# Feed-forward weights of two turns converted, and a third turn's loaded, in the stage before

## What is computed

```
x = layernorm(x + L0_attn(x))             # a two-directional state space mixer
x = layernorm(x + L0_xattn(x, ctx))       # cross attention, 16 query heads, 4 key heads of 96
x = layernorm(x + L0_ffn(x))              # gated feed-forward, quantized weights
x = layernorm(x + L1_attn(x))             # causal self attention, 32 heads of 16
x = layernorm(x + L1_xattn(x, ctx))       # cross attention, 32 query heads, 8 key heads of 128
x = layernorm(x + L1_ffn(x))              # linear layer with routed low-rank terms

def L0_ffn(x):                            # 512 -> 1792 -> 512, scales in groups of 128 rows
    W = (imatrix - zeros) * scales        # for gate, up and down; integers 0 to 15
    return (silu(x @ W_gate) * (x @ W_up)) @ W_down
```

## Time and profile before

| | |
|---|---|
| median of 3 runs | 1649.45 us (1648.58 to 1652.18) |
| the profiled execution, its own time | 1650.77 us |
| its span, from the first to the last instruction | 1649.0 us |
| granted clock of TensorE, mean | 0.983 |
| first cross attention, main loop | about 247 to 527 us |
| feed-forward stage | about 528 to 754 us |

### The profile page before, as it was taken

One profiled execution on the slowest core, in us unless ns is written; L12 is line 12 of the kernel. 1 busy time (PEld: TensorE's weight loads), 2 busy tenths in 40 slices (PEclk: granted clock), 3 DMA queues, 4 the chain that ended last, 5 costly groups with the idle time before them and its releaser, 6 DMA issues. The chain is left out here.

```text
span 1649.0 us, 29540 instructions
## 1 busy us (share of the span) xinstructions
PE 1552.9 (94%) x10984; PEld 1290.7 (78%) x10984; DVE 951.0 (58%) x1693; ACT 798.9 (48%) x2426; POOL 768.0 (47%) x624
## 2 busy tenths in 40 slices
PE   6999999999998779998999889999999999999997
PEld 4777888888886557876777678888888888888875
DVE  3947503333356777778677835555555555555656
ACT  3342324444443445445988734454455445445532
POOL 3403215343321779763533527655455545554413
PEclk9999999999999899999999999999999999999999
DMA  6100200010101743204000021201101011010001
GB/s 211 39 1 1 58 20 21 21 38 5 53 1 46 230 134 128 90 1 122 1 2 27 27 91 39 65 26 39 35 31 52 17 49 39 27 33 14 1 1 51
DMA packets 61777, 77.84 MB, mean 47 GB/s; under 512 B 12168, under 2 KB 41348, under 8 KB 61636
## 3 DMA queue, kind: packets, MB, share of 16 engines
q1 hardware_dynamic: 61172, 74.63, 14.4%
q0 software_dynamic: 464, 1.32, 0.3%
HBM read 73.85 MB, written 2.10 MB: 46 GB/s over the span
## 5 line engine op out<-in xcount | busy, mean ns | idle before, releaser
L1152 POOL TENSOR_TENSOR xa_rs<-xa_ms,minus_half 128x5 f32<-128x5 f32 x64 | 74.8, 1168 | 160.5 <-DVE xa_ms L1423 160.3
L1158 POOL TENSOR_TENSOR xa_prob<-xa_prob,xa_inv 128x512 f32<-128x512 f32 x64 | 66.7, 1042 | 139.0 <-DVE xa_inv L1390 139.0
L766 POOL TENSOR_TENSOR xa_prob<-xa_prob,xa_inv 128x1024 f32<-128x1024 f32 x32 | 60.7, 1895 | 140.8 <-DVE xa_inv L1029 140.8
L1418 DVE TENSOR_REDUCE xa_ssq<-pre 128x4 f32<-128x512 f32 x64 | 43.9, 686 | 134.4 <-ACT pre L1354 134.4
L1368 ACT ACTIVATE xa_prob<-xa_prob,xa_peak 128x128 f32<-128x128 f32 x256 | 99.7, 391 | 41.9 <-DVE xa_peak L1434 41.9
L101 PE MATMUL late_bank<-late_q_hi,xT_hi 128*128 128x512 f32 x284 | 117.9, 415 | 0.0
L1745 DVE SCALAR_TENSOR_TENSOR ff_acc<-ff_ring,ff_sT,ff_acc 128x512 f32<-128x512 f32 x140 | 100.6, 747 | 21.1 <-ACT ff_acc L1699 14.5
L103 PE MATMUL late_bank<-late_q_lo,xT_hi 128*128 128x512 f32 x284 | 112.6, 397 | 0.0
L102 PE MATMUL late_bank<-late_q_hi,xT_lo 128*128 128x512 f32 x284 | 112.5, 396 | 0.0
L1354 ACT ACTIVATE pre<-late_bank 128x512 f32<-128x512 f32 x64 | 38.2, 597 | 141.3 <-PE late_bank L103 141.3
L1985 POOL TENSOR_TENSOR pre<-pre,sa_inv 128x1024 f32<-128x1024 f32 x32 | 63.7, 1989 | 92.0 <-DVE sa_inv L2192 92.0
(11 more groups left out here) (414 smaller groups left out, 4929.9 us busy)
## 6 DMA issues: line engine op xcount, KB each, us to landing
pre<-in_wq SPq DMA_DIRECT2D x8, 1024.0 KB, 5.7
late_raw_o<-in_wo SPq DMA_DIRECT2D x8, 1024.0 KB, 5.3
ff_dn_q<-in_down_w SPq DMA_DIRECT2D x7, 512.0 KB, 3.9
ff_dn_z<-in_down_z SPq DMA_DIRECT2D x7, 512.0 KB, 5.0
ff_dn_s<-in_down_s SPq DMA_DIRECT2D x7, 512.0 KB, 5.8
pre<-in_wq SPq DMA_DIRECT2D x16, 192.0 KB, 3.4
pre<-in_wo SPq DMA_DIRECT2D x16, 192.0 KB, 3.8
pre<-in_xT SPq DMA_DIRECT2D x4, 512.0 KB, 8.1
```

Source lines behind the costliest of these rows:

```text
L766: pool.tensor_tensor(prob[:, t % 3, :, :], prob[:, t % 3, :, :], bc(inv[:, t % 3, :], 2, [P, Q, KEYS]), ALU.mult).then_inc(s["norm"], 1)
L1152: pool.tensor_tensor(rs[:, :], ms[:, :], m.minus_half[:, 0:Q + 1], ALU.pow).then_inc(s["rs"], 1)
L1158: pool.tensor_tensor(prob[:, u % 2, :, :], prob[:, u % 2, :, :], bc(inv[:, u % 2, :], 2, [P, Q, S]), ALU.mult).then_inc(s["norm"], 1)
```

## The change

Two buffers of 8 KB per partition, `early.w`, are allocated for the two stages together. In the cross attention they hold what `q_hi` (and a part of `q_lo`) and one slot of `wide_hi` held; as soon as these are no longer read, DVE converts turns 0 and 1 of the feed-forward weights into them (steps 24, 25 and 28, 29). SP loads turns 0, 1 and 2 one after the other into `pre`. In the feed-forward stage the two buffers are two of the three slots of `w`. Its start loads turn 3 into `other`, the conversions of turns 0 and 1 are gone, those of turns 2 and 3 stand some units earlier, down step 2 stands in units 7 and 8, output row 7 in unit 6, and in SP's loop the load of turn T + 3 stands behind down step T and ahead of down step T + 1.

```diff
+class Early:
+    def __init__(self, sb):
+        self.w = [sb(f"early_w{n}", [P, KC * 2 * WIDE], F32R) for n in range(2)]
...
+    WEIGHTS_AT = ((24, 24, 25, 25), (28, 28, 29, 29))
...
-        wide_hi, wide_lo = (sb(n, [P, 2, SLOT], F32R) for n in ("wide_hi", "wide_lo"))
-        k_hi, k_lo, v_hi, v_lo = (w[:, n, :].rearrange("p (c n) -> p c n", c=KC) for n in range(2) for w in (wide_hi, wide_lo))
-        q0_hi, q0_lo = (sb(n, [P, SLOT], F32R) for n in ("q_hi", "q_lo"))
+        wide_hi = [sb("wide_hi", [P, SLOT], F32R)[:, :], m.early.w[1][:, 0:SLOT]]
+        wide_lo = [sb(f"wide_lo{n}", [P, SLOT], F32R)[:, :] for n in range(2)]
...
+        q_rest = sb("q_lo", [P, SLOT - FEATS], F32R)
+        q0 = pieces(m.early.w[0][:, 0:SLOT + FEATS]) + pieces(q_rest)
...
-                ffn_stage_inputs(sp, io, *ffn_stage_buffer(m.pre), 0, s["ld_next"])
-                sp.wait_ge(s["ld_next"], 96)
+                for T in range(3):
+                    if T:
+                        sp.wait_ge(s["w"], KC * T)
+                    ffn_stage_inputs(sp, io, *ffn_stage_buffer(m.pre), T, s["ld_w"])
+                sp.wait_ge(s["ld_next"], 32)
+                sp.wait_ge(s["ld_w"], 64 * 3)
...
+                def weights(T, c):
+                    q, z = ffn_stage_buffer(m.pre)
+                    if c == 0:
+                        dve.wait_ge(s["ld_w"], 64 * (T + 1))
+                        if T == 0:
+                            dve.wait_ge(s["q_mm"], 3 * B)
+                        else:
+                            dve.wait_ge(s["rows"], 3 * B)
+                    dve.tensor_tensor(ffn_weights(m.early.w[T])[:, c, :, :], q[:, c, :, :], z[:, c, :, :], ALU.subtract).then_inc(s["w"], 1)
...
+                    for T in range(2):
+                        for c in range(KC):
+                            if WEIGHTS_AT[T][c] == t:
+                                weights(T, c)
...
-        w = sb("w", [P, 3, KC, 2, WIDE], F32R)
+        w = [ffn_weights(x) for x in (*m.early.w, sb("w", [P, KC * 2 * WIDE], F32R))]
...
-        mid = {3: [0, 1], 4: [2, 3], 5: [4, 5], 6: [6], 7: [7], **{n: [n - 1] for n in range(9, 22)}, 22: [22], 23: [24, 25], 24: [26, 27],
+        mid = {3: [0, 1], 4: [2, 3], 5: [4, 5], 6: [6, 7], **{n: [n - 1] for n in range(9, 22)}, 22: [22], 23: [24, 25], 24: [26, 27],
...
-        weight_units = {1: (1, 2, 2, 2), 2: (4, 4, 5, 5), 3: (7, 8, 9, 10), 4: (10, 11, 12, 13), 5: (14, 15, 16, 17), 6: (18, 19, 20, 21)}
-        down_units = {0: (1, 1, 1, 2, 2, 2), 1: (3, 3, 4, 5, 5, 6), 2: (6, 6, 7, 7, 7, 8), 3: (10, 10, 11, 12, 12, 13),
+        weight_units = {2: (3, 4, 4, 5), 3: (6, 7, 8, 9), 4: (10, 11, 12, 13), 5: (14, 15, 16, 17), 6: (18, 19, 20, 21)}
+        down_units = {0: (1, 1, 1, 2, 2, 2), 1: (3, 3, 4, 5, 5, 6), 2: (7, 7, 7, 8, 8, 8), 3: (10, 10, 11, 12, 12, 13),
...
                 for T in range(TURNS):
-                    if 0 < T < TURNS - 1:
-                        if T >= 2:
-                            sp.wait_ge(s["w"], KC * (T - 1))
-                        else:
-                            sp.wait_ge(s["w_first"], KC)
-                        ffn_stage_inputs(sp, io, *stage[(T + 1) % 2], T + 1, s["ld_even" if T % 2 else "ld_odd"])
                     if T:
                         sp.wait_ge(s["dn_sub"], T)
                         sp.wait_ge(s["dn_w"], MT * T)
...
-                    if T == 0:
-                        ffn_stage_inputs(sp, io, *stage[1], 1, s["ld_odd"])
+                    if T + 3 < TURNS:
+                        if T:
+                            sp.wait_ge(s["w"], KC * T)
+                        ffn_stage_inputs(sp, io, *stage[(T + 3) % 2], T + 3, s["ld_even" if T % 2 else "ld_odd"])
...
-                q, z = stage[0]
-                for c in range(KC):
-                    dve.tensor_tensor(w[:, 0, c, :, :], q[:, c, :, :], z[:, c, :, :], ALU.subtract).then_inc(s["w_first"], 1)
```

More of the change, by code:

```diff
@@ L649, in cross0_stage, with pieces @@
         SLOT = KC * FEATS
+        def pieces(flat):
+            return [flat[:, n:n + FEATS] for n in range(0, flat.shape[1], FEATS)]
         raw_k, raw_v = (m.pre[:, n * SLOT:(n + 1) * SLOT].rearrange("p (c n) -> p c n", c=KC) for n in range(2))
@@ L675, in wq @@
         def wq(i):
-            hi, lo = (q0_hi, q0_lo) if i % 2 == 0 else (spare_hi, spare_lo)
-            return [w[:, 0:SLOT].rearrange("p (c n) -> p c n", c=KC) for w in (hi, lo)]
+            return (q0[0:KC], q0[KC:2 * KC]) if i % 2 == 0 else [pieces(w[:, 0:SLOT]) for w in (spare_hi, spare_lo)]
         def wo(i):
-            return [w[:, 1 - i % 2, :].rearrange("p (j n) -> p j n", j=BLOCKS) for w in (wide_hi, wide_lo)]
+            return [w[1 - i % 2].rearrange("p (j n) -> p j n", j=BLOCKS) for w in (wide_hi, wide_lo)]
         def mixed(w, c):
@@ L1515, in ffn0_stage @@
         s = {n: sem("ff_" + n) for n in (
[L1516 removed]
+            "ld_even", "ld_odd", "ld_dn", "ld_next", "w", "sT_mm", "sT", "grp", "ca", "cd", "sum", "silu", "h", "h_hi", "h_lo",
             "dn_sub", "dn_w", "dn_hi", "dn_lo", "rows", "add")}
         n2 = norm_sems(sem, "n2")
[L1520 removed]
+        mid = {3: [0, 1], 4: [2, 3], 5: [4, 5], 6: [6, 7], **{n: [n - 1] for n in range(9, 22)}, 22: [22], 23: [24, 25], 24: [26, 27],
                25: [28, 29], 26: [30, 31], 27: [32, 33]}
@@ L1644, in group @@
                     bank = ring[q % RING]
-                    pe.matmul(bank[:, :], w[:, T % 3, c, a, f], m.xT_hi[:, c, cols], start=True, stop=False)
-                    pe.matmul(bank[:, :], w[:, T % 3, c, a, f], m.xT_lo[:, c, cols], start=False, stop=True).then_inc(s["grp"], 1)
+                    pe.matmul(bank[:, :], w[T % 3][:, c, a, f], m.xT_hi[:, c, cols], start=True, stop=False)
+                    pe.matmul(bank[:, :], w[T % 3][:, c, a, f], m.xT_lo[:, c, cols], start=False, stop=True).then_inc(s["grp"], 1)
                 def out_rows(r):
@@ L1673, in _ @@
                     hb, k = TABLE[n]
-                    if n and hb % 2 == 0 and k % MT == 0:
-                        pe.wait_ge(s["w"], KC * turn_of(n))
+                    if turn_of(n) >= 2 and hb % 2 == 0 and k % MT == 0:
+                        pe.wait_ge(s["w"], KC * (turn_of(n) - 1))
                     for i in range(4):
-                        if n == 0:
-                            pe.wait_ge(s["w_first"], i + 1)
                         group(n, i)
@@ L1777, in _ @@
                     part(n, 3)
-                    for T in range(1, TURNS):
+                    for T in range(2, TURNS):
                         for c in range(KC):
@@ L2358 @@
 SHARED = 4
+PAIRED = (1, 2)
 def program(nc, io):
@@ L2368, in program @@
         m.scales, m.own = sb("scales", [P, P]), sb("own", [P, HC])
+        pair = ExitStack()
         for n, stage in enumerate(STAGES):
             used = []
+            if n == PAIRED[0]:
+                m.early = Early(lambda name, shape, dt: pair.enter_context(nc.sbuf_tensor(name, shape, dt)))
             if n == SHARED:
@@ L2379, in program @@
             stage(nc, m, io, sem)
+            if n == PAIRED[1]:
+                pair.close()
             if n < len(STAGES) - 1:
```

17 lines of the change are left out of this document (10 added, 7 removed).

## The result

| | before | after |
|---|---|---|
| median | 1649.59 us (1648.39 to 1652.31, 10 runs) | 1654.41 us (1653.33 to 1657.80, 10 runs) |
| ratio | | 1.003, interval 1.002 to 1.004 |
| the profiled execution, its own time | 1650.77 us | 1654.81 us |
| its span | 1649.0 us | 1653.0 us |
| granted clock, mean | 0.983 | 0.982 |

The account below looks back on a forecast made before the run. TensorE, with matmuls in flight 94% of the span, bounds the kernel, so only its gaps count. 4.7 + 1.3 - 6.4 - 0.4 = -0.8: 0.8 us slower, median 1650.2 us, range 1645.5 to 1655.5, no difference that can be told.

Parts of the forecast that it names:

- Part 1: Feed-forward stage's first gap: early conversions spare DVE the load wait, POOL's chain ends at 550.4; gain 4.7 us (3.3 to 5.9).
- Part 2: Down step 2 moved from unit 6 to 7: DVE's wait for POOL goes, POOL releases TensorE 2.4 us earlier (1.0 to 3.5).
- both loads together: A turn load and the down load queued behind it in SP's queue: 12.8 us, range 12.4 to 14.7.
- Part 3: Down loads behind turn loads in SP's queue: 1.3 of 2.4 us remain after down step 3; down step 4 loses 6.4.
- Part 4: First cross attention: the early conversions on DVE delay a values product in step 29; loss 0.4 us (0 to 1.2).
- an estimate of 10.4 us: Both loads by the skill page's fixed 2.0 us plus bytes over 436 GB/s; would make the sum 5.5 us faster, 1643.9.
- down step 3 in Part 3: Load wanted in unit 10, behind turn 5's: lands 611.2, TensorE restarts at 613.7, not 614.96; 1.3 of 2.4 us remain.
- A slower clock after the wait at 598.4 disappears in the same wait: Around down step 3's wait: no cost counted for TensorE running at the lower clock.
- the clock at down step 4: Lower TensorE clock behind the 4.9 us gap in unit 15: another 1.5 us, within the loss of 6.4.
- queue costs as much as at the old opening: Slower rival: both loads take 14.7 us, down step 4 costs 6.8 + 1.5; 4.7 us slower, 1654.2; chance 0.22.
- Loads sooner: Faster rival: both loads take 11.4 us at 422 GB/s, TensorE restarts at 644.7; +3.4 us, 1646.0; chance 0.20.
- the one on the cross attention: Slower rival: conversions in steps 28 and 29 each delay the step by 1.4 us; 1652.6; chance 0.08.

Follow-up runs that it names:

- e9: Changed kernel with down loads issued ahead of the turn loads and down step 2 back in units 6 and 7 (early conversions alone): 1647.1 us, ratio 0.9992.
- e1: Changed kernel with the loads of down steps 2, 3 and 4 issued ahead of the turn loads: 1642.26 us, ratio 0.9956.
- e2: Changed kernel with only down step 4's load issued ahead of its turn load: 1647.3 us, ratio 0.9985.
- e8: Changed kernel with the loads of down steps 3 and 4 ahead of the turn loads, down step 2's still behind: 1642.47 us, ratio 0.9961.
- e4: Kernel before with only down step 2 moved to units 7 and 8 and output row 7 to unit 6: 1646.6 us, ratio 0.9982.
- e5: Changed kernel with 18 idle products on TensorE in unit 15's wait only: 1653.73 us, ratio 1.0018.
- e3: Changed kernel with idle products on TensorE in the waits of units 11 (13) and 15 (18): 1655.46 us, ratio 1.0029.
- e6: Changed kernel with 13 idle products on TensorE in unit 11's wait only: 1655.42 us, ratio 1.0032.

## Why the prediction was right and wrong

By its own steps, in the time of the old trace:

| step | predicted | measured |
|---|---|---|
| Part 1, down product of unit 3 starts | 550.4, gain 4.7 | 550.08, gain 5.0; 3.9 to 5.4 in units 3 to 5 |
| Part 2, released by POOL | 7.1 gained in all | 593.86, 7.0 gained |
| both loads together | 12.8 us (12.4 to 14.7) | 13.6, 13.3, 12.8 |
| Part 3, restart after down step 3 | 6.0 left | 610.19, 4.8 left |
| clock behind that restart | none counted | 1.5 |
| Part 3, gap at down step 4 | 4.9 | 4.77 |
| clock behind it | 1.5 | 2.45 |
| feed-forward stage in all | 0.4 slower | 4.1 slower |
| Part 4, first cross attention | 0.4 slower | 360.90 and 360.88: none |
| first stage, self attention | unchanged | +1.3, -1.1 |
| second cross attention, last stage | unchanged | -1.5, +1.1 |

**The mechanism was right.** The first gap is gone, and the two behind it, 2.13 and 2.09, are ended by ACT and POOL, not by a load. In e9 POOL's release comes 4.9 us sooner in the stage than before, where Part 1 has 4.7. The wait of 4.24 us for POOL is gone. DVE's two waits for `ff_dn_s` stand in units 10 and 14, and e1, e2 and e8 show that the queue makes them, since nothing else was edited. The Trainium skill's page "DMA: Bandwidth & Descriptors" (the anatomy of one DMA) has the wait on the issuing sequencer before dispatch; the trace agrees, as the issue rows above have every down piece behind the turn load that waited. The same section's 2.0 us plus bytes over 436 GB/s is given there for a single DMA that is issued from POOL, and I had turned it into an estimate of 10.4 us for seven issued from SP. That doesn't agree with the trace: the three pairs took 12.8 to 13.6.

**The step that failed is down step 3 in Part 3**, priced at 1.1 of lost gain where e8 against e2 has 4.1 to 4.6. Three things were wrong in it.
- At the restart 4.8 us of the gain were left and not 6.0: turn 3's last conversion ended about 0.7 later than I had it, and the loads took 13.3.
- The sentence "A slower clock after the wait at 598.4 disappears in the same wait" looked at the clock of the gap before and forgot that of this gap. It is 3.44 us long, between 2.11, after which the earlier trace rows show 1.00, and 4.33, after which they show 0.61, so the rows left it open; I counted nothing, and it was 1.5.
- What the queue costs is measured against what would be without it. There the gap of 1.19 goes too: e8, e1 and e9 have no gap in unit 11, and their lead grows by 1.5 from unit 9 to unit 11, while e4 still shows 1.19 there. The change also moves turn 3's last conversion from unit 10, just ahead of down step 3, to unit 9. I had overlooked this gain. That the conversion makes it is read from the order and wasn't run alone. With the 1.1 of the prediction these three make 5.3 us, which is what lies between after (-7.03 to -3.24) and e8 (-5.79 to -7.27) from unit 9 to unit 11. How much of it is lost depends on the execution: e5, with the same order, had the gap of 1.59 and lost 0.4 there.

**The term that was mis-sized is the clock at down step 4**, 1.5 and not 2.45. I took it from two gaps where TensorE worked off the backlog at the low clock for one window. Here the next window was still at 0.83. With the 1.2 and 1.5 of down step 3 this 0.95 makes 3.65 us, and the stage was off by 3.7.

**Parts 1 and 2 were right in size as well.** At POOL's release the changed kernel has 7.0 us where the prediction has 4.7 + 2.4 = 7.1: 4.9 are there ahead of the moved step (e9 at its release has as much), and 2.1 come by the move, though turn 4's load in front of down step 2 made DVE wait 1.29. Without that wait, in e1, the move gives 2.3, and in e4, alone, 2.8.

**Of the rivals**, "queue costs as much as at the old opening" gave 1654.2, close to the 1654.4 measured, but by another way: it wanted loads of 14.7 us, and they took 12.8 to 13.6. That the number is so near is luck. "Loads sooner" fell with the same numbers, and so did the one on the cross attention, with 360.90 and 360.88 us. Its conversions lie where DVE had time:

```profile
L1034 DVE TENSOR_TENSOR early_w<-pre x8: 677/679/1007, 449.5 to 494.3; 128x512 fp32r<-128x512 int32 x8
its engine sat idle before it (us, times) until:
```

Behind "its engine sat idle before it" no row follows: none of the eight waited for its load. One values product did stand 0.21 us for DVE's low half at 496.89; the stage got it back.

The totals lag behind the stage. For e1, e4 and e9 the stage gained 9.9, 5.6 and 4.9 us and the medians 7.3, 2.8 and 1.7. The spans of the profiled executions are 8.8, 3.8 and 2.9 us shorter than the 1649.0 before, mostly because the first stage was 1.1 to 1.3 longer in them. The rest, 1.0 to 1.5, lies in which execution was profiled: the one of the kernel before took 1650.77 us and its medians in these comparisons were 1649.55, 1649.41 and 1648.83. What stays open is why the unchanged stages scatter. Over all profiles but e3's and e6's, the first cross attention took 360.9 us each time, the first stage 167.0 to 169.2, the self attention 208.4 to 211.2, the second cross attention 650.6 to 652.1 and the last stage 31.1 to 32.3.

## What to carry to other kernels

A load that waits for a buffer holds up every load behind it in its queue, so when a change puts it further ahead, look at what is queued behind it and by when that is wanted; the order of issue should follow the order of need. Here the order turned a change that loses 4.8 us into one that gains 5 to 7, with no other edit. And where TensorE stands as long as it does here (3.4 and 4.8 us), price the slower clock behind the gap too (1.5 and 2.45 us), at the gap that goes as at the one that comes. To tell whether an edit did something in a stage of a kernel whose clock moves about, measure from the last operation ahead of what was edited, not from the stage's start. By the stages the move of down step 2 looks like 5 us or more, and it is 2 to 3.
